# Post-norm decoder layer on one core: decays of sequence 1 one z block later, y of position 0 between the last two z blocks, and GpSimd's gate/up split one step ahead of a token sum

## The chip, the core and the metric

The kernel runs on one core of one Trainium2 chip. The metric is the device time of one execution in microseconds (us). Three runs of the kernel before took 395.16, 395.36 and 396.1 us; their median, 395.36 us, is the time before. PE is the engine that multiplies matrices, DVE the vector engine, ACT the scalar engine, POOL is GpSimd, and SP issues the input transfers.

## The reference, cut to what matters

Eight sequences of 128 tokens with 512 features go through a Mamba-2 block with a gated MLP, an attention over a context, and a routed feed-forward; each of the three ends in a layer norm. The part that the change touches is the Mamba-2 block and the start of its MLP:

```python
h = rmsnorm(hidden_states, ln1_w)
# mamba2: z, xs, Bs, Cs, dt = split(h @ w_in.T); causal conv over 4 taps, silu
dt = jax.nn.softplus(dt + dt_bias); a = dt * A; cs = jnp.cumsum(a, axis=-1)
Ldec = jnp.where(tri, jnp.exp(cs[..., :, None] - cs[..., None, :]), 0.0)
att = jnp.einsum('bchqn,bchkn->bchqk', Cc, Bc) * Ldec
Y = jnp.einsum('bchqk,bchkp->bchqp', att, Xdt) + D[:, None] * xh
h = res + (Y * silu(z)) @ w_out.T
h2 = rmsnorm(h, ln2_w)
h = h + silu(h2 @ gate_w.T) * (h2 @ up_w.T) @ down_w.T
```

A sequence has one chunk of 128 tokens, so no state is carried from chunk to chunk. All products count in fp32: a matrix is split into a high and a low part, and one product is three matmuls (high·low, high·high, low·high).

## The kernel before, in words

Every engine has its own instruction list, written out by hand; semaphores order the lists among each other. What an engine does next is what stands next in its list, even if that waits and something behind it could run.

**In projection.** `in_proj(n)` for n = 0 to 21 multiplies half of the tokens (512) with one 128-column block of the weights: 12 matmuls of 512 columns (L655, L656, L657). N_DVE_IP is 14. The blocks n = 14 to 21 are z, and ACT takes each out of its PSUM bank with `z_silu(n - 14)` (L1139), which counts `z_done` up. The z blocks use banks 4, 7, 2, 3 and so on in turn; n = 19 has bank 7.

**Decays, scores, y.** For position b, that is sequence b of the eight, `decays_of(b)` on PE writes the differences of the running sums into bank 0 or 1 (L709, L711) and then transposes x and the time steps into bank 5 (L719, L720). The transposes wait for `xb_ok` of position b-1, since ACT has to have read bank 5. ACT's `decay(b)` copies bank 5 out (L1145, `xb_ok`) and takes four exponentials (L1149). `scores_of(b)` (L726) fills bank 6, DVE's `att(b)` multiplies scores and decays (L1569), POOL's `skip(b)` adds the skip term (L540), `y_of(b)` on PE (L735) writes y into bank 7. The y of position 0 waits for `z_done` 6: block n = 19 must have left bank 7. What the change calls "decays of sequence 1" is `decays_of(1)`.

**The loop over positions.** In round b PE runs y(b), decays(b+2), the transposes of the normed rows of position b-3 (`turn_h2`, L757), the out projection of b-1 (12 matmuls) and the scores of b+2. DVE runs `gate_y(b)` (y times silu of z, L1577), `low_y(b)` (L1583), `low_h2(b-3)` (L1589), `norm2(b-2)` (L1612), `add_h(b-1)` (L1607) and `att(b+2)`. ACT runs `hi_of_y(b)` (L1154), `hi_of_h2(b-3)` (L1167), `decay(b+2)`, `f32_of_h2(b-3)` (L1171) and the squares and the root for the norm of b-1 (L1065, L1072, L1074). POOL runs `skip(b+2)` and `residual(b-1)` (L544). `norm2` of a position waits for its residual.

**Into the MLP.** `lo_part(n)` on POOL (L487) makes the low part of weight chunk n; GU_CHUNK and GU_CHUNK + 1 are the two chunks of the first gate and up products. `token_sums(i)` (L552, L553, L556, L558) makes the sums of token blocks for a fast matrix product that follows, ACT's `hi_of_t(i)` (L1180) and POOL's `t_low(i)` (L562) split them. PE's first product of the second chunk, `gate_up(1, 0, (0,))`, waits for `lo_part(GU_CHUNK + 1)` and for `f32_of_h2(5)`, which frees bank 4. Between its halves stand `turn_h2(6)` and `turn_h2(7)`; behind them a `half_block` waits for `low_h2(6)`. From there on the seven-product scheme (`strassen`) runs; its second product waits for the split sums (DVE L1653) and all `t_low`.

Of the kernel before, what the change touches and what calls it, by code (L numbers as in the profile page):

```python
# [30 lines left out]
B = 8  # L31
# [3 lines left out]
HB = B // 2  # L35
H = 4
# [8 lines left out]
N_IN = 11  # L45
N_CONV = 6
IN_CHUNKS = (N_IN + 1) // 2
OUT_CHUNK = IN_CHUNKS
GU_CHUNK = OUT_CHUNK + 2
# [45 lines left out]
def last_of_chunk(n):  # L95

    return max(i for i, (m, hf) in enumerate(IN_ORDER) if m // 2 == n)


def raw_slot(n):  # L100

    return n % RAW if n < LOOP_CHUNK else (n - LOOP_CHUNK) % RAW
# [32 lines left out]
def build(nc, x, ctx, ctxT, wstream, conv_w, conv_b, a_log, d_skip, dt_bias, ln1_w, ln2_w,  # L135
          gate_lora, expert_bias, lora_b, out):
    es = ExitStack()
    with es:
# [3 lines left out]
        def sem(name):  # L142
            return es.enter_context(nc.semaphore(name))
# [22 lines left out]
        ringS = station_t[:, 3 * CH:7 * CH].rearrange("p (b s n) -> p b s n", b=2, s=2)  # L166
# [108 lines left out]
        ip_done, z_done = sem("ip_done"), sem("z_done")  # L275
# [9 lines left out]
        sq2, lr2, rs2, hn2 = sem("sq2"), sem("lr2"), sem("rs2"), sem("hn2")  # L285
# [41 lines left out]
        def h2_rows(t):  # L327

            if t < B - 2:
                first = T3 if t % 2 else T1  # L330
                return sets[:, first:first + 2, 0, :, bass.ts(t // 2, P)]
            return tmp[:, bass.ds((4 + t - (B - 2)) * D, D)].rearrange("p (g c q) -> p g c q", g=2, c=2)
# [14 lines left out]
        def t_rows(i):  # L347

            return sets[:, T1:T4 + 1, 1, :, bass.ts(i, P)]

        def t_cols(i, part):

            return setsS[:, T1:T4 + 1, part, :, bass.ts(i, P)]
# [111 lines left out]
        def _(pool):  # L465
# [19 lines left out]
            def lo_part(n, dst, hi):  # L485
                pool.wait_ge(w_hi, n + 1)
                pool.tensor_tensor(dst, raw[:, raw_slot(n), :], hi.bitcast(F32), ALU.subtract).then_inc(w_lo, 1)  # L487
# [46 lines left out]
            def skip(b):  # L534

                d = dec[:, b % 2, :, :]
                if b == 0:
                    pool.wait_ge(vec_setup, 2)
                pool.wait_ge(att_ok, H * (b + 1))
                pool.tensor_tensor(d, d, dI, ALU.add).then_inc(attd_ok, 1)  # L540
# [5 lines left out]
            def token_sums(i, parts=(0, 1)):  # L546

                even, odd, f = h2_rows(2 * i), h2_rows(2 * i + 1), t_rows(i)
                b11, b21, b12, b22 = even[:, 0, :, :], even[:, 1, :, :], odd[:, 0, :, :], odd[:, 1, :, :]
                if 0 in parts:  # L550
                    pool.wait_ge(h2_f32, 2 * i + 2)
                    pool.tensor_tensor(f[:, 0, :, :], b12, b11, ALU.subtract).then_inc(tp_step, 1)  # L552
                    pool.tensor_tensor(f[:, 2, :, :], b22, b12, ALU.subtract).then_inc(tp_step, 1)  # L553
                if 1 in parts:
                    pool.wait_ge(tp_step, 3 * i + 2)
                    pool.tensor_tensor(f[:, 1, :, :], b22, f[:, 0, :, :], ALU.subtract).then_inc(tp_step, 1)  # L556
                    pool.wait_ge(tp_step, 3 * i + 3)
                    pool.tensor_tensor(f[:, 3, :, :], f[:, 1, :, :], b21, ALU.subtract).then_inc(t_f32p, 1)  # L558

            def t_low(i):  # L560
                pool.wait_ge(t_hi, i + 1)
                pool.tensor_tensor(t_cols(i, 1), t_rows(i), t_cols(i, 0).bitcast(F32), ALU.subtract).then_inc(t_lo, 1)  # L562
# [6 lines left out]
            for b in range(B + 1):  # L569
                if b + 2 < B:  # L570
                    skip(b + 2)
                if b >= 1:
                    residual(b - 1)
                if b == 5:
                    token_sums(0, (0,))
                if b == 6:
                    token_sums(0, (1,))
                    token_sums(1)
                if b == 7:
                    lo_part(GU_CHUNK + 1, ringS[:, 1, 1, :], ringS[:, 1, 0, :])  # L580
                    t_low(0)

            def weight_sums(g):

# [55 lines left out]
        N_DVE_IP = 2 + 2 * N_CONV  # L640
# [19 lines left out]
        def _(pe):  # L660
# [61 lines left out]
            def scores_of(b):  # L722

                if b >= 1:
                    pe.wait_ge(att_ok, H * b)
                pe.matmul(bank[6][:, :], bT[:, tok(b)], cT[:, :, tok(b)], start=True, stop=True).then_inc(s1_done, 1)  # L726
# [77 lines left out]
            turn_h(7)  # L804
            in_proj(3)

            decays_after = {N_DVE_IP + 3: 0, N_DVE_IP + 4: 1}
            scores_after = {N_DVE_IP + 3: 0, N_DVE_IP + 6: 1}
            for n in range(4, 2 * N_IN):
                in_proj(n)  # L810
                if n in decays_after:
                    decays_of(decays_after[n])
                if n in scores_after:
                    scores_of(scores_after[n])
            for b in range(B + 1):
                if b < B:
                    y_of(b)
                if b < B - 2:
                    decays_of(b + 2)
                if b == B - 1:  # L820

                    pe.wait_ge(w_lo, GU_CHUNK + 1)
                    pe.wait_ge(h2_lo, HB)
                    gate_up(0, 0, (0,))
                if b == B:
                    gate_up(0, 0, (1,))
                if b >= 3:
                    turn_h2(b - 3)
                if b >= 1:
                    out_proj(b - 1)  # L830
                if b < B - 2:
                    scores_of(b + 2)
# [220 lines left out]
        def _(act):  # L1053
            def hi_part(n, dst):

                act.wait_ge(raw_in[raw_slot(n)], landed(n))
                act.activation(dst, raw[:, raw_slot(n), :], ACT.Copy).then_inc(w_hi, 1)  # L1057
# [178 lines left out]
            for i in range(2):  # L1236
                hi_part(OUT_CHUNK + i, sideS[:, 0, bass.ts(i, CH)])
            decay(1)
            for i in range(4, 2 * H):
                z_silu(i)  # L1240
                if i == 5:
                    act.wait_ge(ip_done, last_of_chunk(IN_CHUNKS - 2) + 1)
                    hi_part(GU_CHUNK, ringS[:, 0, 0, :])
            act.preload_act_table_set(LN_EXP)
            for b in range(B + 1):
                if b < B:
                    hi_of_y(b)
                if b >= 3:
                    hi_of_h2(b - 3)
                if b + 2 < B:  # L1250
                    decay(b + 2)
                if b >= 3:
                    f32_of_h2(b - 3)
                if b == B:
                    hi_of_t(1)
                if b >= 1:
                    norm2(b - 1)
                if b == B - 1:
                    hi_of_t(0)
                if b == 6:  # L1260
                    hi_part(GU_CHUNK + 1, ringS[:, 1, 0, :])
# [204 lines left out]
        def _(v):  # L1466
# [106 lines left out]
            def gate_y(b):  # L1573
                v.wait_ge(y_ps, b + 1)
                if b == 0:
                    v.wait_ge(z_done, 2 * H)
                v.tensor_tensor(blocks(hn[:, b % 2, :]), blocks(bank[7][:, :]), szT[:, :, tok(b)], ALU.mult) \  # L1577
                    .then_inc(y_gated, 1)
# [401 lines left out]
```

## Time and profile before

| what | us |
|---|---|
| median of three runs | 395.36 |
| the profiled execution | 395.69 |
| its span, first to last instruction | 393.9 |
| PE busy | 381.2 (97%) |
| PE weight load busy | 309.8 (79%) |
| DVE busy | 284.2 (72%) |
| ACT busy | 193.0 (49%) |
| POOL busy | 152.8 (39%) |

The chain that ended last lies for 67% of the span on PE, 16% on DVE, 6% on POOL and 4% on ACT. The granted clock of PE is 0.995 of full over the span. A busy share is an average over the whole program; the timeline tells where PE stands still. In a timeline row the columns are the start in us from the start of the span, the duration in us, the engine, the line of the code, the operation, what it writes and reads, and in brackets the idle time ahead of it with what ended it. Matmuls overlap, so the distance from one start to the next says how long PE is taken up, not the printed duration.

### The profile page before, as it was taken

How to read it: one execution, taken by the hardware profiler on the slowest of the kernel's cores; microseconds unless marked ns; L12 is line 12 of the kernel's file. 1: busy time of each engine (PE TensorE's matmuls, PEld its weight loads, DVE VectorE, ACT ScalarE, POOL GpSimd, SP SyncE). 2: the span in 40 equal slices, each digit the busy share in tenths (PEclk: the TensorE clock that was granted, in tenths of full speed). 3: DMA queues.
4: the chain of work that ended last, by engine and by line, in shares of the span. 5: the costliest groups of instructions: out<-in, count | busy, mean ns of one | idle time of the engine just before them, and what ended most of it. 6: DMA issues, size and time to landing. Idle time of an engine off the chain costs nothing.

```text
span 393.9 us, 5382 instructions
## 1 busy us (share of the span) xinstructions
PE 381.2 (97%) x1923; PEld 309.8 (79%) x1927; DVE 284.2 (72%) x501; ACT 193.0 (49%) x390; POOL 152.8 (39%) x139
## 2 busy tenths in 40 slices
PE   8999998999999999999999999999999999999983
PEld 3878886766688998888888888878788888897862
DVE  5599891267764987979797979695666756676575
ACT  7868767866757544242424243863314144142241
POOL 6407325944499732838283837850000000000000
PEclk9999999999999999999999999999999999999998
DMA  8901110110001033120212111451110120101002
GB/s 272 317 3 54 55 53 6 48 55 0 2 0 55 1 114 121 36 99 20 94 33 75 56 53 53 140 175 59 55 54 28 54 82 27 53 27 53 27 2 81
DMA packets 11659, 25.52 MB, mean 65 GB/s; under 512 B 1681, under 2 KB 1809, under 8 KB 11634
## 3 DMA queue, kind: packets, MB, share of 16 engines
q1 hardware_dynamic: 10480, 23.10, 17.8%
q10 hardware_dynamic: 1154, 2.10, 1.4%
q8 instruction: 14, 0.23, 0.3%
q14 instruction: 11, 0.09, 0.1%
HBM read 23.10 MB, written 2.10 MB: 64 GB/s over the span
## 4 chain that ended last, share of the span: by engine, by line
PE 67%; DVE 16%; POOL 6%; ACT 4%; issue 4%; DMA 2%; SPq 0%; DVEq 0%; ACTq 0%
PE bank_first L655 8%; PE bank_first L657 8%; PE bank_first L656 8%; PE bank L655 7%; PE bank L657 7%; PE bank L656 6%; DVE big L1533 5%; PE bank_last L655 5%; PE bank_last L657 5%; PE bank_last L656 5%; PE bank L924 2%; POOL rows L544 2%; PE bank L935 2%; DMA raw<-wstream 2%; DVE sets L1670 1%
## 5 line engine op out<-in xcount | busy, mean ns | idle before, releaser
L655 PE MATMUL bank_first<-sets,station 128*128 128x512 f32 (+1 forms) x172 | 69.9, 406 | 0.1
L655 PE MATMUL bank<-sets,station 128*128 128x512 f32 (+1 forms) x180 | 67.2, 373 | 1.1 <-POOL station L491 0.6
L656 PE MATMUL bank<-sets,station 128*128 128x512 f32 (+1 forms) x180 | 65.8, 366 | 0.0
L657 PE MATMUL bank<-sets,station 128*128 128x512 f32 (+1 forms) x180 | 65.8, 366 | 0.0
L657 PE MATMUL bank_first<-sets,station 128*128 128x512 f32 (+1 forms) x172 | 65.6, 381 | 0.0
L656 PE MATMUL bank_first<-sets,station 128*128 128x512 f32 (+1 forms) x172 | 65.4, 380 | 0.0
L655 PEld LDWEIGHTS bank<-sets,station 128*128 128x128 f32 x180 | 33.9, 188 | 7.8 <-POOL station L487 1.0
L655 PEld LDWEIGHTS bank_first<-sets,station 128*128 128x128 f32 x172 | 32.5, 189 | 8.4 <-issue 2.8
L656 PEld LDWEIGHTS bank<-sets,station 128*128 128x128 f32 x180 | 34.0, 189 | 5.9 <-issue 0.5
L657 PEld LDWEIGHTS bank<-sets,station 128*128 128x128 f32 x180 | 34.0, 189 | 5.5
L656 PEld LDWEIGHTS bank_first<-sets,station 128*128 128x128 f32 x172 | 32.4, 189 | 6.8 <-issue 1.7
L657 PEld LDWEIGHTS bank_first<-sets,station 128*128 128x128 f32 x172 | 32.3, 188 | 6.3
L607 POOL TENSOR_TENSOR big<-tmp,side_f 128x512 f32<-128x512 f32 x17 | 26.5, 1572 | 24.7 <-DVE side_f L1659 24.7
L1377 ACT ACTIVATE small<-small 128x1 f32<-128x1 f32 x24 | 7.1, 295 | 46.2 <-DVE small L1778 46.2
L655 PE MATMUL bank_last<-sets,station 128*128 128x512 f32 (+1 forms) x76 | 28.0, 368 | 0.0
L657 PE MATMUL bank_last<-sets,station 128*128 128x512 f32 (+1 forms) x76 | 27.9, 367 | 0.0
L656 PE MATMUL bank_last<-sets,station 128*128 128x512 f32 (+1 forms) x76 | 27.9, 367 | 0.0
L487 POOL TENSOR_TENSOR station<-raw,station 128x1024 fp32r<-128x1024 f32 x7 | 16.7, 2391 | 25.8 <-ACT station L1057 25.8
L1643 DVE TENSOR_TENSOR station<-raw,station 128x512 fp32r<-128x512 f32 (+1 forms) x24 | 19.0, 832 | 6.1 <-ACT station L1280 6.1
L1280 ACT ACTIVATE station<-raw 128x512 fp32r<-128x512 f32 x12 | 7.5, 625 | 29.8 <-PE bank L657 17.9
L1653 DVE TENSOR_TENSOR station<-side_f,station 128x512 fp32r<-128x512 f32 x24 | 19.4, 814 | 2.1 <-ACT station L1288 2.1
L1533 DVE SCALAR_TENSOR_TENSOR big<-bank,cw,big 128x508 f32<-128x508 f32 (+2 forms) x27 | 19.7, 739 | 0.9 <-ACT big L1127 0.3
(247 smaller groups left out, 864.2 us busy)
## 6 DMA issues: line engine op xcount, KB each, us to landing
raw<-wstream SPq DMA_DIRECT2D x31, 512.0 KB, 3.6
rows<-x SPq DMA_DIRECT2D x8, 256.0 KB, 4.7
big<-ctxT SPq DMA_DIRECT2D x8, 256.0 KB, 2.7
big<-ctx SPq DMA_DIRECT2D x8, 256.0 KB, 3.0
out<-tmp ACTq DMA_DIRECT2D x8, 256.0 KB, 2.0
big<-ln_w SPq DMA_DIRECT2D x1, 256.0 KB, 5.0
big<-lora_b SPq DMA_DIRECT2D x3, 64.0 KB, 4.8
ga<-gate_lora SPq DMA_DIRECT2D x1, 72.0 KB, 4.9
```

The source lines that it names most:

```text
L487: pool.tensor_tensor(dst, raw[:, raw_slot(n), :], hi.bitcast(F32), ALU.subtract).then_inc(w_lo, 1)
L544: pool.tensor_tensor(rows[:, b, :], rows[:, b, :], acc[:, b % 2, :], ALU.add).then_inc(hx_ok, 1)
L607: pool.tensor_tensor(hid_block(m, hf), blocks(sg[:, k, :]), blocks(value), ALU.mult).then_inc(up_ok, 1)
L655: pe.matmul(ps, a_hi, b_lo, start=first, stop=False)
L656: pe.matmul(ps, a_hi, b_hi, start=False, stop=False)
L657: return pe.matmul(ps, a_lo, b_hi, start=False, stop=last)
L924: mm = pe.matmul(bank[4][:, 0:P], qT[:, bass.ts(c, P)], blocks(keyT)[:, c, :], start=(c == 0), stop=(c == DC - 1))
L935: pe.matmul(bank[5][:, :], exT, key, start=True, stop=True).then_inc(pv_ps, 1)
L1280: act.activation(groupS[:, buf, 0, 0:D], raw[:, raw_slot(n), 0:D], ACT.Copy).then_inc(g_hi, 1)
L1533: v.scalar_tensor_tensor(out=dst[:, :, s:L], in0=src[:, :, 0:L - s], scalar=cw[:, m, 3 - s:4 - s], in1=dst[:, :, s:L], op0=ALU.mult, op1=A ...
L1643: v.tensor_tensor(groupS[:, buf, 1, lo:hi], src, groupS[:, buf, 0, lo:hi].bitcast(F32), ALU.subtract) \
L1653: v.tensor_tensor(groupS[:, buf, 1, q], sums[:, bass.ts(k, D)], groupS[:, buf, 0, q].bitcast(F32), ALU.subtract).then_inc(g_lo, 1)
```

## The change: what it does

On PE `decays_of(1)` moves from behind z block 18 to behind z block 19, and `y_of(0)` from behind block 21 to between blocks 20 and 21, behind `scores_of(1)`. ACT's list follows: the high part of chunk GU_CHUNK is taken after the silu of block 20 rather than of block 19, and `hi_of_y(0)` stands ahead of the last silu and of the table load behind it. DVE's `gate_y(0)` waits for seven silus of z, and `gate_y(4)` for the eighth. On POOL `lo_part(GU_CHUNK + 1)` moves ahead of `token_sums(1)` and of `residual(6)`, `token_sums(1)` goes to round 7, and `t_low(0)` stands behind `residual(7)` and waits for the last `norm2`.

```diff
                 if b == 6:
                     token_sums(0, (1,))
+                    lo_part(GU_CHUNK + 1, ringS[:, 1, 1, :], ringS[:, 1, 0, :])
+                if b == 7:
                     token_sums(1)
-                if b == 7:
-                    lo_part(GU_CHUNK + 1, ringS[:, 1, 1, :], ringS[:, 1, 0, :])
-                    t_low(0)
+            pool.wait_ge(hn2, B)
+            t_low(0)
...
-            decays_after = {N_DVE_IP + 3: 0, N_DVE_IP + 4: 1}
+            decays_after = {N_DVE_IP + 3: 0, N_DVE_IP + 5: 1}
...
+                if n == 2 * N_IN - 2:
+                    y_of(0)
             for b in range(B + 1):
-                if b < B:
+                if 0 < b < B:
                     y_of(b)
...
-            for i in range(4, 2 * H):
+            for i in range(4, 2 * H - 1):
                 z_silu(i)
-                if i == 5:
-                    act.wait_ge(ip_done, last_of_chunk(IN_CHUNKS - 2) + 1)
-                    hi_part(GU_CHUNK, ringS[:, 0, 0, :])
+            act.wait_ge(ip_done, last_of_chunk(IN_CHUNKS - 2) + 1)
+            hi_part(GU_CHUNK, ringS[:, 0, 0, :])
+            hi_of_y(0)
+            z_silu(2 * H - 1)
             act.preload_act_table_set(LN_EXP)
...
                 if b == 0:
+                    v.wait_ge(z_done, 2 * H - 1)
+                if b == HB:
                     v.wait_ge(z_done, 2 * H)
```

PE, from z block 18 to the start of the loop over positions. Of each z block (12 matmuls) only the first row stands: bank4 is block 18, bank_last block 19, bank2 block 20 and bank3 block 21. Before:

```order
L655 MATMUL bank4<-sets_49,station_51 128x512 [waits z_done,hT_lo,w_lo]
...
L709 MATMUL bank_first<-big,identb 128x512 [waits rows_ok]
L711 MATMUL bank_first<-cs3_56,tmp 128x128 x4
L719 MATMUL bank5<-ident,big 128x128 [waits xb_ok,cv_done]
L720 MATMUL bank5<-ident,big 128x128
L655 MATMUL bank_last<-sets_49,station_51 128x512 [waits z_done,hT_lo,w_lo]
...
L655 MATMUL bank2<-sets_49,station_51 128x512 [waits z_done,hT_lo,w_lo]
...
L726 MATMUL bank_last<-big 128x512 [waits att_ok]
L655 MATMUL bank3<-sets_49,station_51 128x512 [waits z_done,hT_lo,w_lo]
...
L735 MATMUL bank_last<-big 128x512 [waits z_done,xb_ok,attd_ok]
```

The same stretch with the change (its lines there are one higher):

```order
L656 MATMUL bank4<-sets_49,station_51 128x512 [waits z_done,hT_lo,w_lo]
...
L656 MATMUL bank_last<-sets_49,station_51 128x512 [waits z_done,hT_lo,w_lo]
...
L710 MATMUL bank_first<-big,identb 128x512 [waits rows_ok]
L712 MATMUL bank_first<-cs3_56,tmp 128x128 x4
L720 MATMUL bank5<-ident,big 128x128 [waits xb_ok,cv_done]
L721 MATMUL bank5<-ident,big 128x128
L656 MATMUL bank2<-sets_49,station_51 128x512 [waits z_done,hT_lo,w_lo]
...
L727 MATMUL bank_last<-big 128x512 [waits att_ok]
L736 MATMUL bank_last<-big 128x512 [waits z_done,xb_ok,attd_ok]
L656 MATMUL bank3<-sets_49,station_51 128x512 [waits z_done,hT_lo,w_lo]
```

The four instructions of `decays_of(1)` now follow block 19, and y of position 0, with its three waits, stands ahead of block 21.

POOL at the end of the loop over positions; L544 is a residual, L552 to L558 are token sums, L487 is the low part of chunk GU_CHUNK + 1, L562 is a `t_low`. Before:

```order
L544 TENSOR_TENSOR rows<-rows,tmp 128x512 [waits h_ok]
L556 TENSOR_TENSOR sets_f32_50<-sets_f32_50 128x2x128 [waits tp_step]
L558 TENSOR_TENSOR sets_f32_50<-sets_f32_50 128x2x128 [waits tp_step]
L552 TENSOR_TENSOR sets_f32_50<-sets_f32_50 128x2x128 [waits h2_f32]
L553 TENSOR_TENSOR sets_f32_50<-sets_f32_50 128x2x128
L556 TENSOR_TENSOR sets_f32_50<-sets_f32_50 128x2x128 [waits tp_step]
L558 TENSOR_TENSOR sets_f32_50<-sets_f32_50 128x2x128 [waits tp_step]
L544 TENSOR_TENSOR rows<-rows,tmp 128x512 [waits h_ok]
L487 TENSOR_TENSOR station_51<-raw_54,station_51 128x1024 [waits w_hi]
L562 TENSOR_TENSOR sets_49<-sets_f32_50,sets_49 128x4x2x128 [waits t_hi]
L544 TENSOR_TENSOR rows<-rows,tmp 128x512 [waits h_ok]
L562 TENSOR_TENSOR sets_49<-sets_f32_50,sets_49 128x4x2x128 [waits t_hi]
```

The same stretch with the change:

```order
L544 TENSOR_TENSOR rows<-rows,tmp 128x512 [waits h_ok]
L556 TENSOR_TENSOR sets_f32_50<-sets_f32_50 128x2x128 [waits tp_step]
L558 TENSOR_TENSOR sets_f32_50<-sets_f32_50 128x2x128 [waits tp_step]
L487 TENSOR_TENSOR station_51<-raw_54,station_51 128x1024 [waits w_hi]
L544 TENSOR_TENSOR rows<-rows,tmp 128x512 [waits h_ok]
L552 TENSOR_TENSOR sets_f32_50<-sets_f32_50 128x2x128 [waits h2_f32]
L553 TENSOR_TENSOR sets_f32_50<-sets_f32_50 128x2x128
L556 TENSOR_TENSOR sets_f32_50<-sets_f32_50 128x2x128 [waits tp_step]
L558 TENSOR_TENSOR sets_f32_50<-sets_f32_50 128x2x128 [waits tp_step]
L544 TENSOR_TENSOR rows<-rows,tmp 128x512 [waits h_ok]
L562 TENSOR_TENSOR sets_49<-sets_f32_50,sets_49 128x4x2x128 [waits t_hi,hn2]
L562 TENSOR_TENSOR sets_49<-sets_f32_50,sets_49 128x4x2x128 [waits t_hi]
```

The low part of the chunk moved ahead of five instructions, and the first `t_low` behind the last residual, with a wait for the last norm (`hn2`).

## Rows read from the trace of the kernel before

**Rows 1.** Timeline of PE (columns as told above), z blocks 18 to 21.

```profile
65.14 0.39 PE L709 MATMUL bank_first<-big,identb 128*128 128x512 bf16 x1
...
66.97 0.30 PE L719 MATMUL bank<-ident,big 128*128 128x128 f32 x1 [1.22 <-ACT big L1145]
...
69.97 0.39 PE L655 MATMUL bank<-sets,station 128*128 128x512 f32 x1
...
72.70 1.02 PE L726 MATMUL bank_last<-big 128*128 128x512 f32 x2
...
76.32 1.02 PE L735 MATMUL bank_last<-big 128*128 128x512 f32 x2
```

**Rows 2.** Timeline of ACT, the same stretch.

```profile
66.52 0.31 ACT L1145 ACTIVATE big<-bank 128x164 f32<-128x164 f32 x1
...
71.29 1.28 ACT L1139 ACT_TABLE_LOAD   x1
...
73.08 0.59 ACT L1139 ACTIVATE big<-bank_last 128x512 f32<-128x512 f32 x1
...
76.52 0.60 ACT L1139 ACTIVATE big<-bank 128x512 f32<-128x512 f32 x1 [1.42 <-PE bank L657]
...
78.43 0.63 ACT L1154 ACTIVATE station<-tmp 128x512 fp32r<-128x512 f32 x1
78.97 0.29 ACT L1145 ACTIVATE big<-bank 128x164 f32<-128x164 f32 x1
```

**Rows 3.** Timeline of DVE: low_h2(3).

```profile
109.78 0.68 DVE L1589 TENSOR_TENSOR sets<-bank,sets 128x512 fp32r<-128x512 f32 x1
```

**Rows 4.** Timeline of PE: first matmul of the MLP.

```profile
110.61 0.35 PE L655 MATMUL bank_first<-sets,station 128*128 128x256 f32 x1
```

**Rows 5.** Timeline of POOL, end of the loop over positions.

```profile
115.69 1.27 POOL L552 TENSOR_TENSOR sets_f<-sets_f 128x256 f32<-128x256 f32 x1
...
121.07 2.40 POOL L487 TENSOR_TENSOR station<-raw,station 128x1024 fp32r<-128x1024 f32 x1
...
127.48 2.40 POOL L562 TENSOR_TENSOR sets<-sets_f,sets 128x1024 fp32r<-128x1024 f32 x1
```

**Rows 6.** Timeline of DVE, the same stretch.

```profile
115.67 0.69 DVE L1583 TENSOR_TENSOR station<-tmp,station 128x512 fp32r<-128x512 f32 x1 [2.23 <-ACT station L1154]
...
116.88 0.74 DVE L1612 SCALAR_TENSOR_TENSOR tmp<-tmp,rst,big 128x512 f32<-128x512 f32 x1
...
121.62 2.40 DVE L1612 SCALAR_TENSOR_TENSOR tmp<-tmp,rst,big 128x512 f32<-128x512 f32 x1
...
127.62 2.81 DVE L1612 SCALAR_TENSOR_TENSOR tmp<-tmp,rst,big 128x512 f32<-128x512 f32 x1 [3.01 <-POOL rows L544]
```

**Rows 7.** Timeline of ACT, the same stretch.

```profile
118.26 0.63 ACT L1065 ACTIVATE big<-tmp 128x512 bf16<-128x512 f32 x1 [0.66 <-DVE tmp L1607]
...
119.45 1.04 ACT L1180 ACTIVATE sets<-sets_f 128x1024 fp32r<-128x1024 f32 x1
...
121.73 0.60 ACT L1171 ACTIVATE sets_f<-bank 128x512 f32<-128x512 f32 x1 [0.76 <-DVE sets L1589]
```

**Rows 8.** Timeline of PE, out projection of position 7 to half_block.

```profile
122.58 0.39 PE L657 MATMUL bank<-side,station 128*128 128x512 f32 x1
123.52 0.39 PE L655 MATMUL bank<-sets,station 128*128 128x256 f32 x1 [0.55 <-POOL station L487]
...
130.48 0.66 PE L757 MATMUL bank_last<-ident,tmp 128*128 128x128 f32 x4 [0.52 <-DVE tmp L1612]
131.08 0.39 PE L655 MATMUL bank<-sets,station 128*128 128x256 f32 x1
```

**Rows 9.** Timeline of DVE: second half of the first split sums.

```profile
141.52 0.69 DVE L1653 TENSOR_TENSOR station<-side_f,station 128x512 fp32r<-128x512 f32 x1
```

**Rows 10.** Timeline of PE: the first product of the seven-product scheme.

```profile
142.70 0.40 PE L655 MATMUL bank_first<-sets,station 128*128 128x512 f32 x1
```

**Rows 11.** Stretch 142 to 300 us: us, busy us of PE, PEld, DVE, ACT, POOL.

```profile
142.00:300.00 158.00, 157.85 (x722) 130.39 (x721) 126.37 (x186) 65.89 (x108) 71.96 (x67) 1.00 0.24 77
```

More of the change, by code:

```diff
@@ L1238, in _ @@
             decay(1)
-            for i in range(4, 2 * H):
+            for i in range(4, 2 * H - 1):
                 z_silu(i)
-                if i == 5:
-                    act.wait_ge(ip_done, last_of_chunk(IN_CHUNKS - 2) + 1)
-                    hi_part(GU_CHUNK, ringS[:, 0, 0, :])
+            act.wait_ge(ip_done, last_of_chunk(IN_CHUNKS - 2) + 1)
+            hi_part(GU_CHUNK, ringS[:, 0, 0, :])
+            hi_of_y(0)
+            z_silu(2 * H - 1)
             act.preload_act_table_set(LN_EXP)
             for b in range(B + 1):
-                if b < B:
+                if 0 < b < B:
                     hi_of_y(b)
```

## The prediction

> **What bounds the kernel now.** I read the busy shares first: PE is busy for 97% of the span, so only the moments in which PE stands still, or has more to do, can move the time. The change adds and removes no instruction on any engine; it moves some, and adds waits. So the second view is the stretches, and the third the timeline of PE around the moved places, with the brackets that say how long it was idle and what ended it. From 142 to 300 us PE is busy for 157.85 of 158.00 us [rows 11]: what is won or lost ahead of 142 us is handed on through a full PE, with nothing to absorb it. Behind 300 us the order of all engines is unchanged and starts from PE's products, so I let the shift pass to the end.
>
> The change aims at three standstills of PE. At 66.97 the transposes of the decays of position 1 wait 1.22 us for ACT to empty bank 5 [rows 1]. At 123.52 the second gate chunk waits for POOL's low part. At 130.48 the transposes of position 7 wait 0.52 us for DVE, and the matmuls at 131.08 for the DVE operation behind it [rows 8]. For each I work out whether PE runs on, or what is late next.
>
> **Part 1: decays(1) behind block 19, y(0) ahead of block 21.** A z block takes 2.73 us (69.97 to 72.70); scores and a block together 3.62 us (72.70 to 76.32), so scores 0.89, and y, of the same shape, the same [rows 1]. Before, the group of y(0) ends at 76.32 + 0.89 = 77.21.
>
> After: block 19 starts at 65.14 and ends at 67.87. ACT's bank 5 copy ends at 66.52 + 0.31 = 66.83 [rows 2], so decays(1) no longer waits; without its wait it takes 0.6 to 0.9 us. With block 20 (2.73) and scores(1) (0.89) PE comes to y(0) between 72.1 and 72.4. But y(0) writes bank 7 and waits for ACT to take block 19 out of it. That silu is ACT bound: it stands behind decay(1) and a table load at 71.29, and ends at 73.08 + 0.59 = 73.67 [rows 2]. Nothing ahead of it in ACT's list is moved, and giving it its product 2 us earlier doesn't help. From ACT's end to PE's start the trace has 66.97 - 66.83 = 0.14 us. So y(0) starts at 73.81, after a new wait of 1.4 to 1.7 us, in place of the old 1.22. Then y 0.89 and block 21 2.73: 77.43, against 77.21. **Term 1: +0.22 us.**
>
> What is late next: the last silu waits for block 21, which ended at 76.32 and now ends at 77.43, so it moves from 76.52 to 77.63. Behind it before stood the table load, hi_of_y(0) and decay(2), 2.45 us later at 78.97; hi_of_y(0) (0.54, 78.43 to 78.97) is gone from there [rows 2], which leaves 1.91: decay(2) at 79.54, 0.57 late. From decay(2) the ring att, skip, residual, norm2, add_h, att on DVE and POOL takes its time and keeps the 0.57, while PE is 0.22 late. PE's first MLP matmul waits for low_h2(3), which ended at 109.78 + 0.68 = 110.46 against PE's 110.61 [rows 3, 4]. After: 111.03 and about 0.05 for the semaphore (DVE's 127.62 + 2.81 = 130.43 released PE at 130.48 [rows 6, 8]), 111.08, against 110.61 + 0.22 = 110.83. **Term 2: +0.25 us**, so PE is 0.47 late from there. By bounds, if that ring takes up its lag it is 0, if PE has no slack at all it is 0.35.
>
> **Part 2: POOL's low part ahead of token_sums(1).** PE's last matmul ahead of this chunk starts at 122.58 and takes 0.23 until the next may start: 122.81; it started at 123.52, so 0.71 was lost [rows 8]. After, PE is there at 122.81 + 0.47 = 123.28, and the low part is long done. But the same PE product also waits for f32_of_h2(5), and its chain now runs into POOL.
>
> DVE's norm2, whose inputs are all in SBUF, doesn't run beside a POOL instruction. POOL's low part ran from 121.07 to 123.47 [rows 5]; the norm2 issued at 121.62 took 2.40 us instead of 0.74 and ended at 124.02, 0.55 behind POOL's end [rows 6]. The other way round, low_y at 115.67 took its plain 0.69, and the POOL sum issued at 115.69 took 1.27 [rows 5, 6]. Whoever comes first keeps the other out.
>
> After, the low part takes the place of that sum. All three move by 0.57. Low_y runs from 116.24 to 116.93, the low part behind it to about 119.2. Norm2(5), issued at 116.88 + 0.57 = 117.45, is locked out and ends at 119.2 + 0.55 = 119.75 instead of 117.62. The squares for position 6 came 0.64 behind that end (118.26): 120.39. Behind them, by distances read off the timeline of before [rows 7]: hi_of_t(0) 1.19 later (118.26 to 119.45) at 121.58, f32_of_h2(5) 2.28 behind that (119.45 to 121.73, with hi_of_h2(5) and DVE's low_h2(5) between) at 123.86, its end + 0.60 = 124.46, PE + 0.14 = 124.60. That is 1.3 us behind what PE could do, and 1.08 us later than the 123.52 of before. **Term 3: the low part's wait goes (-0.71), the wait for f32_of_h2(5) takes its place (+1.32).** Bounds: 0 if norm2(5) gets in first, +2.1 if low_y is locked out as well (a rival below).
>
> **Part 3: t_low(0) behind the last norm.** Norm2(7) took 2.81 us at 127.62, since POOL's t_low had the way from 127.48 to 129.88, 0.55 ahead of its end [rows 5, 6]. After, POOL waits for it, and it takes 0.74. Before, it started 4.10 us behind PE's 123.52, held up by its residual, which stood behind the low part and a t_low; now four short sums stand there instead. Even 4.10 behind the new 124.60 it would end by 129.5; I take a start 3 us behind, and its end near 128.3. From 123.52 PE could have been at the transposes at 129.80 (130.48 - 0.52, less the 0.16 by which a modelled end overlaps the next start, 122.97 against 122.81 [rows 8]), 6.28 later; after, it is there at 130.88, and finds norm2(7) and low_h2(6) done. Transposes without a wait take 0.36. The matmuls of 131.08 then start at 124.60 + 6.28 + 0.36 = 131.24. **Term 4: -0.92** (0.68 ahead of the transposes, 0.24 behind).
>
> **Sum** at that matmul: +0.47 - 0.71 + 1.32 - 0.92 = +0.16 us, 131.24 against 131.08. The other moves cost nothing: hi_part(GU_CHUNK) comes 0.5 us later, ready for POOL, which doesn't reach it before; gate_y(0) is far earlier; SP's transfers that wait for the low parts come earlier, never later. The span goes from 393.9 to 394.06 and the profiled execution from 395.69 to 395.85; that execution was 0.33 above the median of the runs, so on the median's scale it is 395.36 + 0.16, **395.5 us**.
>
> **Rivals.**
>
> *POOL wins the race against low_y (0.17).* The order of 115.67 and 115.69 is decided by 0.02 us. The Trainium skill (SBUF — State Buffer, Who interferes with whom) says that of a DVE instruction with two SBUF inputs and a GpSimd instruction that reads SBUF the one issued first fully blocks the other; the trace agrees both ways round (2.40 us for DVE, 1.27 for POOL). If the low part is first, it runs 116.26 to 118.66, low_y ends at 119.21, and low_h2(4) and norm2(5) behind it (115.67 to 116.88 was 1.21, then 0.74) end at 120.5, 0.75 later than in the forecast. All behind it follows: +0.9, 396.3 us.
>
> *POOL's lag reaches the seven-product stage: slower (0.13).* t_low(0) starts near 128.3, and t_low(1), 2.4 us behind it, at 130.7, against 127.48 [rows 5]: up to 3.2 us late, and with it the weight sums that follow in POOL's list, which ACT and DVE split. The split sums of DVE ended at 141.52 + 0.69 = 142.21 [rows 9]; PE's second product needs them at 142.70 + 6 x 0.23 = 144.1 [rows 10], and PE itself comes 0.16 later, so 2.0 us of lag are free; between the ends 0 and 3.2 I take 1.6 for what reaches DVE. At the full 3.2, PE stands for 1.2 us, and the time is 395.5 + 1.2 = 396.7. It decides from a lag of 2.0 us on. For it speaks that POOL is the one engine whose list is pushed back; against it that ACT's own list stood between.
>
> *The cover holds: faster (0.22).* If norm2(5) is issued ahead of the low part, or the lock costs less, f32_of_h2(5) is in time and PE goes on at 123.28: 123.28 + 6.64 = 129.92, -1.16, 394.2 us. A y(0) with a shorter wait would add to it. For it: two of three standstills really go. Against: the low part's inputs are ready at 115.7, 1.8 us ahead of norm2(5).
>
> **How the numbers follow.** The forecast has 0.48. 0.3% is 1.2 us (394.2 and 396.5), about what a measurement of this kernel can tell from no change. Of the faster case half is beyond it, and with an uncounted gain that makes 0.15; of the slower case most, and a little of the race: 0.13; the rest, 0.72, is no change. Range: from the cover case, 394.1, to the lag case, 396.8.
>
> **What would show it.** In the profile after: no wait at the transposes of decays(1); a wait of some 1.6 us of the first y (L736) for ACT's silu; the z stretch ending 0.2 late; the wait of the second gate chunk, now on ACT's L1174, not on POOL, near 124.6; a norm2 of some 2.3 us near 117.5; none at the last transposes, and a last norm2 of 0.75 us; PE's first seven-product matmul 0.16 us later than at 142.70. It is wrong if the first y waits under 1 us, if the gate chunk starts before 124 us, or if a wait appears at the second product.

## The result, and the profile after

The changed kernel takes 396.18 us (median of 19 runs, 395.48 to 398.03); the kernel before took 395.38 us beside it (19 runs, 394.96 to 397.0). The ratio is 1.0019, 95% interval 1.001 to 1.0027: slower, by 0.4 to 1.1 us, and less than 0.3%. Timed again beside three other kernels on another occasion it took 396.19 us against 395.75, ratio 1.0011 (1.0 to 1.0022): slower by 0 to 0.9 us. The profiled execution took 396.27 us; the first two rows of its page are:

```profile
span 394.3 us, 5388 instructions
...
PE 382.4 (97%) x1927; PEld 310.9 (79%) x1927; DVE 284.5 (72%) x501; ACT 193.2 (49%) x390; POOL 152.9 (39%) x139
```

The waits of PE between 60 and 145 us (what waits, for what, total us, times, longest) are two. Before they were the three of [rows 1, 8]; not one of those is left.

```profile
PE bank_last L736 <- ACT big L1142: 1.5, 1, 1.5
PE bank L656 <- ACT sets_f L1174: 1.0, 1, 1.0
```

The timeline of PE at the places of [rows 1, 4, 8, 10]. All starts are 0.13 us late already ahead of the first moved instruction (the first scores of PE start at 61.66, before at 61.53); that part differs from execution to execution.

```profile
73.94 1.10 PE L736 MATMUL bank_last<-big 128*128 128x512 f32 x2 [1.49 <-ACT big L1142]
...
77.64 0.39 PE L710 MATMUL bank_first<-big,identb 128*128 128x512 bf16 x1
...
111.39 0.35 PE L656 MATMUL bank_first<-sets,station 128*128 128x256 f32 x1
...
123.35 0.39 PE L658 MATMUL bank<-side,station 128*128 128x512 f32 x1
124.79 0.35 PE L656 MATMUL bank<-sets,station 128*128 128x256 f32 x1 [1.05 <-ACT sets_f L1174]
...
131.04 0.60 PE L758 MATMUL bank_last<-ident,tmp 128*128 128x128 f32 x4
131.39 0.36 PE L656 MATMUL bank<-sets,station 128*128 128x256 f32 x1
...
142.99 0.40 PE L656 MATMUL bank_first<-sets,station 128*128 128x512 f32 x1
```

PE stands for 1.49 us ahead of y of position 0 and for 1.05 us ahead of the second gate chunk; the last transposes (131.04) and the half_block (131.39) follow without a wait. ACT, at the places of [rows 2, 7]:

```profile
66.66 0.31 ACT L1148 ACTIVATE big<-bank 128x164 f32<-128x164 f32 x1
...
71.42 1.28 ACT L1142 ACT_TABLE_LOAD   x1
...
73.20 0.59 ACT L1142 ACTIVATE big<-bank_last 128x512 f32<-128x512 f32 x1
...
77.84 0.60 ACT L1142 ACTIVATE big<-bank 128x512 f32<-128x512 f32 x1 [1.41 <-PE bank L658]
...
79.75 0.31 ACT L1148 ACTIVATE big<-bank 128x164 f32<-128x164 f32 x1
...
120.57 0.63 ACT L1068 ACTIVATE big<-tmp 128x512 bf16<-128x512 f32 x1 [2.21 <-DVE tmp L1613]
...
121.76 1.05 ACT L1183 ACTIVATE sets<-sets_f 128x1024 fp32r<-128x1024 f32 x1
...
124.05 0.60 ACT L1174 ACTIVATE sets_f<-bank 128x512 f32<-128x512 f32 x1 [0.76 <-DVE sets L1595]
```

The silu of block 19 ends at 73.20 + 0.59 = 73.79 and releases y at 73.94. f32_of_h2(5) ends at 124.65 and releases the gate chunk at 124.79. POOL and DVE, at the places of [rows 5, 6, 9]:

```profile
116.45 2.94 POOL L487 TENSOR_TENSOR station<-raw,station 128x1024 fp32r<-128x1024 f32 x1
...
128.39 4.76 POOL L562 TENSOR_TENSOR sets<-sets_f,sets 128x1024 fp32r<-128x1024 f32 x2 [1.75 <-DVE tmp L1618]
```

```profile
116.44 0.69 DVE L1589 TENSOR_TENSOR station<-tmp,station 128x512 fp32r<-128x512 f32 x1 [2.22 <-ACT station L1157]
...
117.65 2.29 DVE L1618 SCALAR_TENSOR_TENSOR tmp<-tmp,rst,big 128x512 f32<-128x512 f32 x1
...
127.56 0.75 DVE L1618 SCALAR_TENSOR_TENSOR tmp<-tmp,rst,big 128x512 f32<-128x512 f32 x1 [2.29 <-ACT rst L1077]
...
143.50 0.68 DVE L1659 TENSOR_TENSOR station<-side_f,station 128x512 fp32r<-128x512 f32 x1
```

Low_y at 116.44 comes 0.01 us ahead of POOL's low part at 116.45, which then takes 2.94 us instead of 2.40. The norm2 issued at 117.65 (norm2(5), of position 5) is locked out until the low part ends and takes 2.29 us instead of 0.74. The last norm2, for which POOL waits, takes 0.75 instead of the 2.81 of [rows 6]. From 142 to 300 us PE is as full as in [rows 11]:

```profile
142.00:300.00 158.00, 157.85 (x723) 130.35 (x722) 128.54 (x187) 65.55 (x106) 72.14 (x67) 1.00 0.23 77
```

### The profile page after: what moved, and what is told of

Its sections match the earlier page's. It is cut to its first block, busy times and chain, and to the rows that moved or that the text cites. A ratio compares the mean times of both kernels' runs of the same rounds, so it can differ in the third digit from the quotient of the medians.

```text
span 394.3 us, 5388 instructions
## 1 busy us (share of the span) xinstructions
PE 382.4 (97%) x1927; PEld 310.9 (79%) x1927; DVE 284.5 (72%) x501; ACT 193.2 (49%) x390; POOL 152.9 (39%) x139
## 4 chain that ended last, share of the span: by engine, by line
PE 73%; DVE 15%; ACT 6%; issue 3%; POOL 2%; DVEq 0%; ACTq 0%
PE bank_first L656 8%; PE bank_first L658 8%; PE bank_first L657 8%; PE bank L656 7%; PE bank L657 7%; PE bank L658 7%; DVE big L1537 5%; PE bank_last L656 4%; PE bank_last L657 4%; PE bank_last L658 4%; PE bank L927 2%; PE bank L938 2%; PE bank_last L736 1%; PE bank_last L727 1%; DVE sets L1676 1%
## 5 line engine op out<-in xcount | busy, mean ns | idle before, releaser
L487 POOL TENSOR_TENSOR station<-raw,station 128x1024 fp32r<-128x1024 f32 x7 | 17.8, 2541 | 25.7 <-ACT station L1060 25.6
L1649 DVE TENSOR_TENSOR station<-raw,station 128x512 fp32r<-128x512 f32 (+1 forms) x24 | 20.1, 876 | 6.1 <-ACT station L1284 6.1
L1659 DVE TENSOR_TENSOR station<-side_f,station 128x512 fp32r<-128x512 f32 x24 | 21.7, 906 | 2.5 <-ACT station L1292 2.5
L1292 ACT ACTIVATE station<-side_f 128x1024 fp32r<-128x1024 f32 x12 | 12.7, 1057 | 17.5 <-POOL side_f L600 17.5
```

Source lines behind the costliest of these rows:

```text
L1292: act.activation(groupS[:, buf, 0, D + HALF_K:7 * HALF_K], sums, ACT.Copy).then_inc(g_hi, 1)
L1649: v.tensor_tensor(groupS[:, buf, 1, lo:hi], src, groupS[:, buf, 0, lo:hi].bitcast(F32), ALU.subtract) \
L1659: v.tensor_tensor(groupS[:, buf, 1, q], sums[:, bass.ts(k, D)], groupS[:, buf, 0, q].bitcast(F32), ALU.subtract).then_inc(g_lo, 1)
```

## The experiments

The start of an execution scatters. To take it out, the table counts from PE's first scores, which stand ahead of everything that is moved, to four later starts on PE: the second gate chunk, the half_block, the first of the seven products, and the last transposes of the program. "Outside" is the run's time less its span, mean over its timed runs. "Ratio" is against the kernel before, timed beside each run; its four medians go from 395.38 to 395.75 us.

| kernel | gate chunk | half_block | first product | last transposes | outside | median us | ratio (95%) |
|---|---|---|---|---|---|---|---|
| before | 61.99 | 69.55 | 81.17 | 325.90 | 1.83 | 395.38 to 395.75 | 1 |
| changed | 63.13 | 69.73 | 81.33 | 326.15 | 2.01 | 396.18 | 1.0019 (1.001 to 1.0027) |
| changed, again | 63.14 | 69.74 | 81.34 | 326.07 | 2.01 | 396.19 | 1.0011 (1.0 to 1.0022) |
| decays only | 61.23 | 68.80 | 80.42 | 325.19 | 1.83 | 394.82 | 0.9979 (0.997 to 0.9988) |
| first part | 62.63 | 70.20 | 81.81 | 326.61 | 1.81 | 396.11 | 1.0012 (0.9999 to 1.0026) |
| POOL's part | 62.50 | 69.11 | 80.71 | 325.54 | 2.03 | 395.49 | 0.9997 (0.9988 to 1.0006) |
| changed, low_y first | 63.37 | 69.99 | 81.59 | 326.33 | 2.14 | 396.41 | 1.0019 (1.001 to 1.0028) |
| t_low waits | 61.97 | 68.60 | 80.20 | 324.90 | 2.02 | 394.81 | 0.9987 (0.997 to 1.0004) |
| one more wait | 61.71 | 69.27 | 80.89 | 325.66 | 2.04 | 395.66 | 1.0002 (0.9992 to 1.0013) |
| changed, low part behind residual(6) | 61.89 | 69.48 | 81.10 | 326.98 | 2.02 | 397.06 | 1.0032 (1.0016 to 1.0048) |
| changed, split sums | 62.12 | 68.73 | 80.32 | 326.08 | 2.02 | 395.56 | 0.9999 (0.9984 to 1.0015) |
| decays, split sums | 60.62 | 67.16 | 78.76 | 324.06 | 2.01 | 394.23 | 0.9963 (0.9952 to 0.9975) |
| decays, split sums, no wait | 60.67 | 67.22 | 78.81 | 323.54 | 1.81 | 393.33 | 0.9943 (0.993 to 0.9956) |

The distances of the changed kernel, which was profiled twice, agree to 0.01 us as far as the first product and to 0.08 at the last transposes. Those of "one more wait", in which nothing is moved, lie 0.24 to 0.28 below the kernel before. That is no scatter: it has a cause in the trace, told at that run. So a difference between two rows is good to 0.1 us only where both executions took the same course there.

**Decays only.** Of the change only the place of decays(1):

```diff
-            decays_after = {N_DVE_IP + 3: 0, N_DVE_IP + 4: 1}
+            decays_after = {N_DVE_IP + 3: 0, N_DVE_IP + 5: 1}
```

> Only the decays of position 1 are moved behind block 19; y of position 0 and POOL's list stay as before. Theory of the waits: the 1.22 us wait at the transposes goes and y(0) finds bank 7 long free, so PE reaches y(0) at 74.9 instead of 76.3 (1.4 earlier). The out projection of position 0 then waits about 0.7 for low_y(0), whose high part still stands behind ACT's last silu and table load; -0.9 us against the kernel before by the second gate chunk and at the end, 394.5. Rival (what is out of the traces' waits costs the changed kernel 0.5 us whatever is moved): -0.4. Rival (the removed wait was hidden anyway): 0.

Measured: 0.83 us faster than the 395.65 of the kernel before beside it. Its waits on PE:

```profile
PE bank L655 <- DVE station L1583: 0.5, 1, 0.5
PE bank_last L757 <- DVE tmp L1612: 0.5, 1, 0.5
PE bank L655 <- POOL station L487: 0.4, 1, 0.4
```

The wait at the transposes is gone, and half a microsecond comes back at the first out projection (the first row), which waits for low_y(0). By the second gate chunk 0.76 us are left (61.23 against 61.99), where 0.9 was expected. This one line is what pays in the first part.

**The first part of the change, POOL as before.** The edit is the change without its lines in POOL's loop.

> The whole first part (decays, y of position 0, ACT's and DVE's order), with POOL's list as before. Theory of the waits: y(0) waits 1.5 us for ACT, and the loop over positions starts 0.2 late on PE and 0.57 late on DVE and POOL; at the second gate chunk and at the end +0.5 to +0.6 us, since the low part and the last norm come later by POOL's 0.57. Rival (it is PE's lag alone that counts): +0.2. Rival (the first part is free, the loss sits in POOL's part): 0.

Measured: +0.46 us in the median, with an interval that just holds 1, and +0.64 at the first product. PE's waits:

```profile
PE bank_last L735 <- ACT big L1141: 1.5, 1, 1.5
PE bank L655 <- POOL station L487: 0.5, 1, 0.5
PE bank_last L757 <- DVE tmp L1617: 0.5, 1, 0.5
```

Moving y(0) ahead of block 21 takes back what the decays gave, and more: against "decays only" it is 1.3 us slower (396.11 against 394.82). Both waits further down are as long as before. PE is late by the same 0.66 us already at the first matmul of the MLP (110.73 - 60.99 = 49.74 from its scores, before 110.61 - 61.53 = 49.08), as late as the other engines, and the whole lag is handed on.

**POOL's part alone.** The edit is the change's lines in POOL's loop, in the kernel before.

> POOL's list alone as in the change, all else as before. Theory of the waits: norm2(5) is locked out by the low part, so PE waits 1.3 for f32_of_h2(5) at the second gate chunk, which starts at 124.0 (+0.5); the two waits at 130.5 and 131.1 go (-0.9), and the time is 0.5 us shorter, 394.9. Rival (POOL's lag reaches the seven-product stage): a wait of PE at its second product of 0.3 us or more, and -0.2 or worse. Rival (the low part's move pays): the second gate chunk at 122.9, and -1.6.

Measured: -0.16 us, with an interval that holds 1; at the first product -0.46. PE's waits:

```profile
PE bank L720 <- ACT big L1146: 1.2, 1, 1.2
PE bank L656 <- ACT sets_f L1172: 1.1, 1, 1.1
```

On PE it is what the theory said; no wait appears at the second product. In the time 0.5 us was expected: outside the span the run loses 0.20 us, which no theory had, so less is left.

**Is the race lost in the runs that no trace shows?**

```diff
                     token_sums(0, (1,))
+                    pool.wait_ge(y_lo, B)
                     lo_part(GU_CHUNK + 1, ringS[:, 1, 1, :], ringS[:, 1, 0, :])
```

> The changed kernel, with one more wait on POOL: the low part waits for low_y of position 7, so that DVE always has the SBUF port first there. It tells whether the changed kernel loses in some of its executions what its profile doesn't show. Rival of the race (in most timed executions POOL was first, +0.75): the time is 0.5 to 0.7 us under the changed kernel's, +0.2 against before. Theory (the race is won in nearly all of them, the rest of the measured +0.75 is elsewhere): the same as the changed kernel or 0.1 us over it, +0.8 against before.

Measured: 396.41 us, no faster than the changed kernel (396.18 and 396.19). The rival as it was put, that POOL was first in most of the timed executions, falls: forcing DVE to be first would then have gained 0.5 us or more. That POOL is first in a few of them is not excluded, since the forced order has a price of its own: the low part ends 0.24 us later (118.95 - 60.98 = 57.97 from the scores, against 119.39 - 61.66 = 57.73), the gate chunk comes as much later (63.37 against 63.13), and 0.13 us more lie outside the span.

**t_low(0) behind the last norm2, and nothing else.** POOL's loop ends

```diff
                 if b == 7:
                     lo_part(GU_CHUNK + 1, ringS[:, 1, 1, :], ringS[:, 1, 0, :])
-                    t_low(0)
+            pool.wait_ge(hn2, B)
+            t_low(0)
```

> The kernel before with one thing of the change: t_low(0) stands behind residual(7) and waits for the last norm2; the low part stays where it was. Theory of the waits: both waits at the last transposes and the half_block go, no other comes, and the half_block starts 0.9 to 1.1 us earlier after the same start of the decays; with the 0.2 us that the change of POOL's list adds outside the span, 0.8 us faster than before. Rival (t_low(0) is then late for the second product): a wait there and less than 0.4 us won.

Measured: 0.80 us under the kernel before in the median, the forecast value, but with an interval that just holds 1: 4 of its 12 runs lie 0.9 us and more above the others. The profiled one is such a run, and its first scores start at 62.75, 1.2 us later than the 61.53 of before, so in this run the excess is from the start of the execution; the other three have no trace. In the trace the half_block comes 0.95 us earlier (68.60), and the waits are:

```profile
PE bank L720 <- ACT big L1146: 1.2, 1, 1.2
PE bank L656 <- POOL station L487: 0.6, 1, 0.6
```

So of POOL's part this is the half that pays. The other half, the low part moved ahead, adds 0.5 to the gate chunk (62.50 against 61.97).

**Split sums: the low part between the halves of token_sums(1).** With the decays of "decays only":

```diff
                 if b == 6:
                     token_sums(0, (1,))
-                    token_sums(1)
+                    token_sums(1, (0,))
                 if b == 7:
                     lo_part(GU_CHUNK + 1, ringS[:, 1, 1, :], ringS[:, 1, 0, :])
-                    t_low(0)
+                    token_sums(1, (1,))
+            pool.wait_ge(hn2, B)
+            t_low(0)
```

> The decays of position 1 behind block 19 alone, t_low(0) behind the last norm2, and the low part between the two halves of token_sums(1), behind residual(6): norm2(5) is then not locked out, and the low part is done at about 122. Theory of the waits: all three standstills go; what is left is 0.6 us at the first out projection and 0.2 to 0.5 at the second product. 2.0 us faster than before, 393.6. Rival (PE's standstills are only passed on): under 1.2 us faster.

Measured: 1.4 us faster (0.9963) in the time, where 2.0 was expected; 2.4 at the first product, and 1.8 at the last transposes. PE's waits are down to

```profile
PE bank L657 <- DVE station L1585: 0.5, 1, 0.5
PE bank_first L657 <- DVE station L1655: 0.3, 1, 0.3
```

Norm2(5) is not locked out as in the changed kernel, and norm2(6), which took 2.40 us before (121.62 in [rows 6]), hardly is:

```profile
116.31 0.74 DVE L1614 SCALAR_TENSOR_TENSOR tmp<-tmp,rst,big 128x512 f32<-128x512 f32 x1
...
121.06 0.88 DVE L1614 SCALAR_TENSOR_TENSOR tmp<-tmp,rst,big 128x512 f32<-128x512 f32 x1
```

The second product now waits for the split sums: PE has come so early that POOL's lag shows. Counted from start to start this wait costs more than its 0.3: from the first product to the last transposes PE takes 245.30 us, against the 244.73 of before.

**One more wait of POOL.** Nothing moved:

```diff
+            pool.wait_ge(hn2, 1)
             t_low(1)
             weight_sums(G0)
```

> The kernel before with a wait of POOL, long met, ahead of t_low(1), and nothing moved. The kernels with POOL's list changed took 2.0 to 2.1 us outside their span, the others 1.8. Theory (one more instruction in POOL's list costs it): 2.0 outside the span, the span as before, +0.2 us. Rival (it is the new order's last part of the program that ends otherwise): 1.8 outside, 0.

Measured: 2.04 us outside the span, against 1.82 of the kernel before beside it, and the span no longer (mean 393.7 against 393.84). The theory holds for the part outside; the whole time, +0.05 where +0.2 was expected, can't be told from none. The kernel with two more waits of POOL shows 2.14, and all kernels without one 1.81 to 1.83.

This trace also shows a second close race, and it is one of the kernel before: the edit stands behind it. In the profile of before norm2(5), issued at 116.88, went ahead of the POOL sum issued at 116.93, which took 1.29 us. Here the two are issued as close, and POOL is first:

```profile
116.89 0.73 POOL L553 TENSOR_TENSOR sets_f<-sets_f 128x256 f32<-128x256 f32 x1
```

```profile
116.85 1.32 DVE L1613 SCALAR_TENSOR_TENSOR tmp<-tmp,rst,big 128x512 f32<-128x512 f32 x1
```

The norm2 ends 0.55 us later, but POOL comes 0.28 us earlier to residual(6) and to the low part (119.54 against 119.82, 120.80 against 121.07), for which PE waits: these are the 0.28 us by which this row lies under the kernel before. The profiles with that POOL order unchanged as far as there ("decays only", "first part", "t_low waits", "decays, split sums" with and without the wait) all went as the profile of before did. How often the timed executions of the kernel before take the one course or the other, no run here tells.

**The low part behind residual(6), ahead of token_sums(1), in the changed kernel.**

```diff
                 if b == 6:
                     token_sums(0, (1,))
-                    lo_part(GU_CHUNK + 1, ringS[:, 1, 1, :], ringS[:, 1, 0, :])
                 if b == 7:
+                    lo_part(GU_CHUNK + 1, ringS[:, 1, 1, :], ringS[:, 1, 0, :])
                     token_sums(1)
```

> The changed kernel with the low part behind residual(6), ahead of token_sums(1). Norm2(5) isn't locked out, so if its lock-out is the cause of the wait for f32_of_h2(5), the second gate chunk starts without a wait, 1.3 to 1.5 us earlier than in the changed kernel. What is late next: token_sums(1) ends some 2.5 us later, and ACT's hi_of_t(1) and all of POOL's list with it. Theory (POOL's lag is the next bound): waits of about 1 us each at the half_block and at the second product, and 0.3 us slower than the changed kernel. Rival (the lag has slack): 1.3 us faster than the changed kernel.

Measured: 397.06 us, 0.9 us slower than the changed kernel, where 0.3 was expected. The waits:

```profile
PE bank_last L736 <- ACT big L1142: 1.5, 1, 1.5
PE bank_first L656 <- DVE station L1659: 0.8, 1, 0.8
PE bank L656 <- DVE sets L1595: 0.8, 1, 0.8
```

The wait for f32_of_h2(5) is gone and the gate chunk comes 1.24 us earlier (61.89 against 63.13): the lock-out of norm2(5) was its cause. In its place PE waits at the half_block and at the second product. This is the lag that the prediction had as its slower rival; one POOL instruction of 2.4 us in another place calls it up.

**Split sums with the first part of the change.** The same edit of POOL's loop, in the changed kernel.

> The changed kernel with the low part between the halves of token_sums(1), behind residual(6); first part as in the change. Theory of the waits: norm2(5) is not locked out, the second gate chunk and the half_block wait for nothing, and POOL's lag costs 0.8 at the second product; 0.7 us less than the changed kernel, about -0.3 against before with the 0.2 outside the span. The first part of the change (y(0) between the last two blocks) then costs 1.3 to 1.5 us against the same list of POOL with the decays alone moved. Rival (the lock-out is not the cause): the second gate chunk waits 1 us for f32_of_h2(5) as in the changed kernel.

Measured: 395.56, against 395.75 beside it: -0.2 in the medians, where -0.3 was expected, with a ratio (0.9999) that can't be told from 1. The waits are 1.5 at y(0) and 0.7 at the second product, none at the gate chunk. Against "decays, split sums" the first part of the change costs 1.3 us (395.56 against 394.23, timed on two occasions) in the time; by the two traces it is 2.0 at the last transposes, and this difference was not followed up.

**Split sums without the wait.** As "decays, split sums", less `pool.wait_ge(hn2, B)`.

> Decays of position 1 behind block 19 and the low part between the halves of token_sums(1), with t_low(0) behind residual(7) but without the wait for the last norm2. Theory of the waits: t_low(0) then gets the port 2.5 to 3.5 us earlier, the last norm2 is locked out behind it but still ends ahead of PE's transposes, and the wait at the second product goes: 0.3 us less on PE than with the wait. Theory of the extra instruction: 1.8 instead of 2.0 us outside the span. Together 393.7 to 393.9, 1.8 faster than before. Rival (the locked-out norm2 holds PE): a wait at the last transposes of 0.5 us or more, and no gain over the kernel with the wait.

Measured: 393.33 us, ratio 0.9943 (0.993 to 0.9956): 2.4 us faster than the 395.75 beside it, where 1.8 was expected, and faster than both kernels of this case. It has 5 timed runs, the others 11 or more. PE has one wait between 60 and 145 us:

```profile
PE bank L656 <- DVE station L1584: 0.5, 1, 0.5
```

The last norm2 is locked out again, and it doesn't matter:

```profile
125.43 1.88 DVE L1613 SCALAR_TENSOR_TENSOR tmp<-tmp,rst,big 128x512 f32<-128x512 f32 x1 [2.40 <-ACT rst L1075]
```

```profile
128.33 0.60 PE L758 MATMUL bank_last<-ident,tmp 128*128 128x128 f32 x4
```

It ends at 127.31, 1.0 us ahead of PE's transposes. With the residual early enough, keeping POOL off the port costs more (0.5 us by the last transposes, from the wait at the second product, and 0.2 outside the span) than it saves.

**The changed kernel again.**

> The changed kernel itself once more beside these, on the same chip, to narrow its difference to the kernel before. By the forecast's waits +0.2 at the seven-product stage, +0.2 outside the span for the one more wait of POOL: +0.4 to +0.5 us. Rival (something else that the trace of one execution doesn't show): +0.8 again.

Measured: +0.44 us (396.19 against 395.75), the theory's value; the rival's +0.8 is at the far end of the interval (0 to 0.9).

## Why the prediction was right

The forecast was 395.5 us, no change that can be told, and +0.16 on PE. The time is 396.18, inside the range, 0.7 us above the forecast: the change is a little slower, by less than the 0.3% that the forecast called no change. The steps of the forecast, the 0.13 us of the late start taken off each measured time:

- **y(0) waits for ACT.** Forecast start 73.81, measured 73.94 - 0.13 = 73.81. The table load and the silus behind it stood where they stood before. The Trainium skill (ScalarE: Activation LUTs, What ACT_TABLE_LOAD costs) puts a switch of tables at 2.66 us, a load of 1.28 and 1.38 for a drain. The load in this trace takes the 1.28 us, but the next activation starts 1.29 us behind its start (71.42 to 72.71), so here the shorter figure decides.
- **Term 1, +0.22:** y and block 21 took 3.70 us (73.94 to 77.64), not 3.62, and the decays behind them started at 77.51, 0.30 later than the 77.21 that I had put for before. The mechanism is right, the size 0.08 small.
- **Term 2, +0.25:** first MLP matmul at 111.39 - 0.13 = 111.26, 0.65 later than before where the two terms give 0.47. Beyond term 1 that is 0.35, the value that I had as the bound for a PE without slack. It doesn't all arise at that matmul: from the start of the last y ahead of it PE takes 1.02 us (110.37 to 111.39), before 0.80 (109.81 to 110.61), which is 0.22; the other 0.13 gathers in the loop over positions.
- **Term 3:** norm2(5) ended at 119.94 - 0.13 = 119.81 (forecast 119.75), the gate chunk started at 124.66 (124.60). PE stood 1.2 us, counted from 123.35 + 0.23, where I had 1.32, since PE itself came later. "Low part behind residual(6)" shows the cause: without the lock-out the wait is gone.
- **Term 4, -0.92:** the half_block at 131.26 against 131.24. From the gate chunk to the half_block it is 6.60 us instead of 7.56; "t_low waits", with this part alone, gives 6.63.
- **Sum at the half_block:** +0.16 forecast, 131.26 - 131.08 = +0.18 measured, and +0.16 at the first of the seven products (142.86 against 142.70). Terms 1 and 2 don't show in it, in the forecast as in the trace, since PE's lag only shortens the wait for f32_of_h2(5): what ended late was a chain that runs over ACT, DVE and POOL, and PE's own lag was swallowed by the wait at its end.

What the sum lacked is outside the span. I let the 1.79 us around it stand, and the one wait that the change adds to POOL's list makes them 0.18 longer (2.01 against 1.83). With the +0.25 us at the last transposes in the first profile that makes 0.43 us, and with the +0.17 in the second 0.35. This lies near the 0.44 of the second timing and at the lower end of the first one's interval, 0.4 to 1.1.

That the +0.16 on PE was met to 0.02 us is partly luck. It holds against the one profile of before from which it was worked out, in which norm2(5) won its race against a POOL sum. Against "one more wait", where the same list lost it, the changed kernel is 0.44 us later at the first product (81.33 against 80.89) and 0.49 at the last transposes, and with the 0.18 outside that is 0.67 us. The two timings, 0.80 and 0.44, would fit a kernel before that takes now the one course and now the other. That is argued only, since the timed executions have no trace, and the start of an execution scatters by as much.

Of the rivals, the race was as close as put: 0.01 us in this profile. DVE was first in both profiles of the changed kernel, and forcing it to be first gained nothing, so a race lost in most executions is excluded. The lag of POOL was nearer than its chance of 0.13 says. DVE's split sums ended at 143.50 + 0.68 = 144.18, against 142.21 before. Less the late start that is 1.84 us of lag, where I had put 1.6, and of the 2.0 that I had counted as free hardly any were left: PE started its second product at 142.99 + 6 x 0.23 = 144.4. Where PE comes earlier, the wait appears (0.3 and 0.7 us with split sums). The faster rival needed norm2(5) ahead of the low part; by it the gate chunk would have come 1.32 us earlier than in the forecast (123.28 against 124.60), and it came 1.24 earlier when that was arranged. Of its -1.16 at the half_block the changed kernel with split sums had -0.82 (68.73 against 69.55), but the second product took it back.

## What to carry to other kernels

Before an instruction is moved ahead of a wait, look which engine is in the way at the new place: y(0) was pulled in front of a wait for ACT that had been hidden by one more product of PE. An instruction moved on an engine off the critical path is paid through what it keeps out: 2.4 us of POOL made one DVE norm 1.55 us longer (2.29 instead of 0.74), and through it held up PE. Where two engines come to such a lock within 0.05 us of each other, one profile is one of two courses: take a second before trusting 0.3 us. Take such a change apart: here one line of the first part (the decays) was worth 0.8 us, the rest of that part cost 1.3, and the decays together with POOL's low part a few rows later and t_low(0) behind the last residual, without a wait, gained 2.4 us.

## What the runs showed of the hardware

One more wait in POOL's list lengthens the time outside the span by 0.2 us (from 1.83 us to between 2.01 and 2.04, in seven kernels), also where it is long met ("one more wait"); two of them lengthen it by 0.3 (2.14). What in it takes the time no trace shows.

A DVE instruction with both inputs in SBUF and a POOL instruction keep each other out: 2.29 us for a norm of 0.74 (117.65), 2.94 for a low part of 2.40 (116.45). A locked-out norm ends 0.55 us behind POOL's end, less than its own 0.74. The Trainium skill (SBUF — State Buffer, Who interferes with whom) states the rule; that the loser needs less than its own time behind the release is only in these rows. The page also lets the order of issue decide. In these traces it did at 116.44 against 116.45, where DVE came first, but where both waited behind a POOL instruction still running it did not always: with DVE issued 0.04 to 0.05 us ahead, DVE was first in the profile of before (116.88 against 116.93) and POOL in "one more wait" (116.85 against 116.89).
